# One exponential a pair of score banks, with the 16-bit part cast on GpSimd

## What is computed

```python
x = x + attention(group_norm(x))        # layer 0
x = x + likelihood(group_norm(x))       # layer 1
# attention: q, k = prelu(1x1 conv to 24 channels), v = prelu(1x1 conv to 192 channels)
score = softmax(einsum('bnc,bcm->bnm', q, k), axis=2)      # 4096 x 4096 an image
out = einsum('bnm,bmc->bnc', score, v)
# likelihood: a small per-channel network (1-3-3-3-1, tanh) of x - 0.5 and x + 0.5
likelihood = maximum(abs(sigmoid(sign * upper) - sigmoid(sign * lower)), 1e-6)
```

## Time and profile before

| what | value |
|---|---|
| median of 3 runs | 5428.71 us (5420.52 to 5429.87) |
| the profiled execution, its own time | 5432.77 us |
| its span | 5430.7 us |
| mean granted clock of TensorE | 0.942 |
| instructions | 105319 |
| chain of work that ended last, by engine | TensorE 56%, ScalarE 12%, DMA 11%, issue 11%, VectorE 8%, GpSimd 1% |

### The profile page before, as it was taken

How to read it: one execution, slowest core, us unless ns; L and a number is a source line. 1 busy time by engine, 2 the same in 40 slices (tenths; PEclk the granted TensorE clock), 3 DMA queues, 4 the chain that set the end, 5 groups by cost and what they waited for, 6 DMA issues and landing times.

```text
span 5430.7 us, 105319 instructions
## 1 busy us (share of the span) xinstructions
PE 4730.2 (87%) x38408; PEld 3138.7 (58%) x38408; DVE 4132.9 (76%) x5378; ACT 3765.9 (69%) x4149; POOL 805.6 (15%) x934
## 2 busy tenths in 40 slices
PE   4999779998899977999789997899878998789966
PEld 2877327773378723886248762588525885267821
DVE  4887578966888667886678867788577885789855
ACT  1666786667866687666876668766687666876677
POOL 5200320003200132001310013100221002210012
PEclk8999899998999899998999989999899998899988
DMA  2101440014300143001430024200242002420033
GB/s 56 26 19 30 106 110 18 13 38 108 100 18 19 37 117 89 16 19 43 121 81 13 19 56 118 71 19 15 68 120 56 19 19 74 118 53 14 19 99 94
DMA packets 107342, 305.21 MB, mean 56 GB/s; under 512 B 14401, under 2 KB 14785, under 8 KB 105090
## 3 DMA queue, kind: packets, MB, share of 16 engines
q1 hardware_dynamic: 106818, 298.01, 20.6%
HBM read 230.65 MB, written 50.33 MB: 52 GB/s over the span
## 4 chain that ended last, share of the span: by engine, by line
PE 56%; ACT 12%; DMA 11%; issue 11%; DVE 8%; SPq 1%; POOL 1%; DVEq 0%; ACTq 0%; POOLq 0%
PE ps L1270 10%; PE ps L1272 10%; PE ps L1274 10%; DMA arena<-x2d 7%; PE ps L1058 7%; PE ps L1221 6%; ACT th L627 5%; PE ps L1085 4%; ACT arena L620 3%; DVE mxp L958 3%; PE ps L1132 2%; PE ps L1115 2%; PE ps L1146 2%; DMA qst<-shared 2%; DVE arena L953 2%
## 5 line engine op out<-in xcount | busy, mean ns | idle before, releaser
L1272 PE MATMUL ps<-v_sb,arena 128*128 128x192 f16 x8192 | 2039.7, 249 | 0.0
L1270 PE MATMUL ps<-v_sb,arena 128*128 128x193 f16 x8192 | 2031.2, 248 | 8.7 <-DVE arena L953 8.7
L1274 PE MATMUL ps<-v_sb,arena 128*128 128x193 f16 x8192 | 2022.7, 247 | 0.0
L577 ACT ACTIVATE arena<-ps 128x1024 f16<-128x1024 f32 x1024 | 1049.5, 1025 | 1018.2 <-PE ps L1058 1017.9
L953 DVE TENSOR_TENSOR arena<-arena 128x1024 f16<-128x1024 f32 x1024 | 1247.8, 1219 | 281.5 <-ACT arena L580 280.1
L958 DVE TENSOR_REDUCE mxp<-ps 128x1 f32<-128x512 f32 x1792 | 1188.1, 688 | 124.6 <-PE ps L1221 113.2
L900 DVE SCALAR_TENSOR_TENSOR th<-th,gates,ps 128x1024 f32<-128x1024 f32 x768 | 953.7, 1277 | 428.1 <-ACT th L627 426.4
L580 ACT ACTIVATE arena<-ps 128x1024 f32<-128x1024 f32 x1024 | 1045.9, 1021 | 0.0
L1272 PEld LDWEIGHTS ps<-v_sb,arena 128*128 128x128 f16 x8192 | 801.0, 98 | 265.3 <-issue 4.7
L627 ACT ACTIVATE th<-ps,biases 128x1024 f32<-128x1024 f32 x768 | 821.6, 1118 | 158.7 <-PE ps L1132 124.3
L1270 PEld LDWEIGHTS ps<-v_sb,arena 128*128 128x128 f16 x8192 | 798.2, 97 | 145.7 <-issue 22.1
(11 more groups left out here) (122 smaller groups left out, 3528.6 us busy)
## 6 DMA issues: line engine op xcount, KB each, us to landing
arena<-x2d SPq DMA_DIRECT2D x384, 256.0 KB
arena<-x2d SPq DMA_DIRECT2D x384, 128.0 KB, 3.8
xp<-x_dram SPq DMA_DIRECT2D x18, 1536.0 KB, 15.2
shared<-x_dram SPq DMA_DIRECT2D x64, 384.0 KB, 3.6
x2d<-shared SPq DMA_DIRECT2D x64, 384.0 KB, 3.1
res<-x2d SPq DMA_DIRECT2D x96, 256.0 KB
out_dram<-res SPq DMA_DIRECT2D x96, 256.0 KB
kst<-shared SPq DMA_DIRECT2D x32, 256.0 KB, 11.2
```

Source lines behind the costliest of these rows:

```text
L577: act.activation(e_hi[:, q % 4, :].rearrange("p (k n) -> p k n", k=2), sc, ACT.Exp)
L1270: pe.matmul(acc, eh, v_sb[:, m, 0:C + 1], start=(m == 0 and t % 2 == 0), stop=False, skip_group_check=True)
L1272: pe.matmul(acc[:, 0:C], eh, v_sb[:, m, VW:VW + C], start=False, stop=False, skip_group_check=True)
L1274: ins = pe.matmul(acc, el, v_sb[:, m, 0:C + 1], start=False, stop=(m == MT - 1), skip_group_check=True)
```

## The change

ScalarE takes one exponential of each pair, the 32-bit one, into `e_32`, which now has four slots (`ER`). GpSimd reads it and writes the 16-bit part `e_hi` with a cast (`high`). GpSimd now has a `phase_b` of its own. It waits for the exponential (`full_ready`) and, from the fifth pair on, for the pair four before to be used up (`summed`); it signals `hi_ready`. VectorE's `low` waits for `hi_ready` instead of `full_ready`. ScalarE waits for `lo_ready` of the pair four before only. TensorE's program is unchanged: it waits for `full_ready` and `lo_ready` at the same places. The three steps of the last layer-1 unit on GpSimd move from the end of its phase A to pairs 1, 3 and 5 of its new phase B, each behind the cast of that pair.

```diff
+ER = 4
...
-        e_32 = arena[:, 8 * N:12 * N].rearrange("p (s n) -> p s n", s=2)
+        e_32 = arena[:, 8 * N:16 * N].rearrange("p (s n) -> p s n", s=ER)
...
@@ GpSimd, phase_a @@
-                    if l is not None and 0 <= u < UNITS:
+                    if l is not None and 0 <= u < (UNITS - 1 if proj else UNITS):
...
+            def high(pairs, q):
+
+                full, free = pool.compute_val(pairs + (q + 1)), pool.compute_val(pairs + (q - 3))
+                settle(pool)
+                pool.wait_ge(full_ready, full)
+                if q >= 4:
+                    pool.wait_ge(summed, free)
+                pool.tensor_copy(e_hi[:, q % 4, :], e_32[:, q % ER, :]).then_inc(hi_ready, 1)
+
+            def phase_b(b, l):
+                def body(before, first, final):
+                    pairs = pool.compute_val(b * BLOCKS * PAIRS + before * PAIRS)
+                    for p in range(PAIRS):
+                        if p + 2 < PAIRS or not final:
+                            high(pairs, (0 if first else PAIRS) + p + 2)
+                        if first and l is not None:
+                            if p == 1:
+                                sums(l, UNITS - 1)
+                            if p == 3:
+                                signs(l, UNITS - 1)
+                            if p == 5:
+                                difference(l, UNITS - 1)
+
+                for q in range(2):
+                    high(pool.compute_val(b * BLOCKS * PAIRS), q)
+                body(0, True, False)
+                with pool.Fori(0, (BLOCKS - 2) // 2) as jj:
+                    body(pool.compute_val(jj * 2), False, False)
+                    body(pool.compute_val(jj * 2 + 1), False, False)
+                body(BLOCKS - 2, False, True)
...
@@ ScalarE, exps @@
-                if q >= 4:
-                    act.wait_ge(summed, pairs + (q - 3))
-                act.activation(e_hi[:, q % 4, :].rearrange("p (k n) -> p k n", k=2), sc, ACT.Exp)
-                if q >= 2:
-                    act.wait_ge(lo_ready, pairs + (q - 1))
-                act.activation(e_32[:, q % 2, :].rearrange("p (k n) -> p k n", k=2), sc,
+                if q >= ER:
+                    act.wait_ge(lo_ready, pairs + (q - ER + 1))
+                act.activation(e_32[:, q % ER, :].rearrange("p (k n) -> p k n", k=2), sc,
                                ACT.Exp).then_inc(full_ready, 1)
...
@@ VectorE, low @@
-                    dve.wait_ge(full_ready, pairs + (q + 1))
-                    dve.tensor_tensor(e_lo[:, q % 4, :], e_32[:, q % 2, :], e_hi[:, q % 4, :],
+                    dve.wait_ge(hi_ready, pairs + (q + 1))
+                    dve.tensor_tensor(e_lo[:, q % 4, :], e_32[:, q % ER, :], e_hi[:, q % 4, :],
                                       ALU.subtract).then_inc(lo_ready, 1)
```

More of the change, by code:

```diff
@@ L242, in program @@
         full_ready = sem("full_ready")
+        hi_ready = sem("hi_ready")
         lo_ready = sem("lo_ready")
@@ L481, in coefficients, with sums, signs, difference @@
                 ins.then_inc(set_gp, 1)
+            def sums(l, u):
+                pool.wait_ge(lu_ready, l * UNITS + u + 1)
+                if u >= 1:
+                    pool.wait_ge(signed_ready, l * UNITS + u)
+                pool.tensor_tensor(lu_sign[:, :], lu[:, u % 2, 0, :], lu[:, u % 2, 1, :], ALU.add
+                                   ).then_inc(sum_ready, 1)
+            def signs(l, u):
+                pool.wait_ge(sign_ready, l * UNITS + u + 1)
+                pool.tensor_tensor(lu[:, u % 2, 0, :], lu[:, u % 2, 0, :], lu_sign[:, :], ALU.mult)
+                pool.tensor_tensor(lu[:, u % 2, 1, :], lu[:, u % 2, 1, :], lu_sign[:, :], ALU.mult
+                                   ).then_inc(signed_ready, 1)
+            def difference(l, u):
+                pool.wait_ge(sig_ready, l * UNITS + u + 1)
+                pool.tensor_tensor(lu[:, u % 2, 0, :], lu[:, u % 2, 1, :], lu[:, u % 2, 0, :], ALU.subtract
+                                   ).then_inc(dif_ready, 1)
             def phase_a(l, proj):
@@ L503, in values @@
                                        ALU.subtract).then_inc(v_done, 1)
[L505 to L521, removed]
                 if proj:
@@ L531, in phase_a @@
                     u = (s - 5) // 4
-                    if l is not None and 0 <= u < UNITS:
+                    if l is not None and 0 <= u < (UNITS - 1 if proj else UNITS):
                         if (s - 5) % 4 == 0:
-                            sums(u)
+                            sums(l, u)
                         if (s - 5) % 4 == 1:
-                            signs(u)
+                            signs(l, u)
                         if (s - 5) % 4 == 2:
-                            difference(u)
+                            difference(l, u)
+            def high(pairs, q):
[25 more added lines that the diff above has]
+                body(BLOCKS - 2, False, True)
             phase_a(None, True)
             coefficients()
-            with pool.Fori(0, B - 1) as b:
-                phase_a(b, True)
+            phase_b(0, None)
+            with pool.Fori(0, B - 1) as l:
+                phase_a(l, True)
+                phase_b(pool.compute_val(l + 1), l)
             phase_a(B - 1, False)
```

## The result

The changed kernel takes 5523.4 us (median of 4 runs, 5519.9 to 5526.9) against 5426.4 us before: ratio 1.018, 95% interval 1.0162 to 1.0197. That is outside the range of 5429 to 5470 us and 3.6 times the loss of 27 us that was forecast.

What follows compares the result with a forecast made beforehand. TensorE, not ScalarE, was taken as the bound in attention, with VectorE also full in pairs with maxima. 8 x 1.0 + 7 x 0.9 + 8 x 1.6 = 27.1 us gave 5459.9 us profiled, 5455 us median; range 5429 to 5470 us.

Steps and rivals of the forecast that it cites:

- Cast 1.03 us: The added 128x1024 cast on GpSimd takes 1.03 us, extrapolated from smaller casts; 2.0 us kept as the other bound.
- Full pairs unchanged, cover of the chain 0.8 us: Pairs with three maxima stay 3.08 us apart; in pairs without maxima the longer exponential-to-low chain has 0.8 us to spare.
- In short pairs, cast plus low want 2.25 us of 2.43 us: tight, but it fits: In pairs without maxima, the port shared by VectorE and GpSimd has room for cast and low; no loss.
- What is queued in front of the cast on GpSimd: Sum, sign products and difference of the last unit stand between casts; low, then TensorE's products, wait for the cast.
- (b): First block with a previous image, 7 times: low 5 meets GpSimd's second sign product, +0.9 us each.
- (a): Start of phase B, 8 times: cast 1 takes the port before low 0, +1.0 us each; otherwise +0.1 us.
- (c): Last block after the square root's table loads, 8 times: cast 9 goes before low 8, +1.6 us; otherwise +0.4 us.
- Low up to 2.2 us, TensorE behind low near 25 us: Signs: low's maximum rises from 1.41 us, some 20 to 30 times; TensorE's wait for low rises from 8.7 us.
- Port throughput in short pairs: Rival, chance 0.10: casts nearer 1.5 us overfill pairs without maxima, 118 us at most, about 5500 us.
- Low ahead: Rival, chance 0.25: low takes the port before the cast at phase B's start and in last blocks; 10.3 us, 5439.
- no change: Rival, chance 0.12: the port costs nothing, as sign products fall differently or VectorE's four-maxima pairs have slack; 5429 to 5433.
- Faster: Rival, chance 0.08: at phase B's start and in last blocks TensorE gains the removed exponential's 0.9 us; 14 us, 5414.

Runs made afterwards that it cites:

- middle: Changed kernel, GpSimd's cast of pair 13 held back, both exponentials on ScalarE in every image's first and last blocks (last: pairs 2 to 15): 5416.7 us, ratio 0.9999.
- wait13: Changed kernel, with GpSimd's cast of pair 13 held back until the maxima are split, in all blocks but an image's last: 5496.3 us, ratio 1.0125.
- idle casts: Kernel before, plus on GpSimd a 960-column cast of a constant tile per pair that nobody waits for: 5453.6 us, ratio 1.0056.
- first block: Changed kernel, with both exponentials on ScalarE for pairs 0 to 15 of image 0 alone: 5494.9 us, ratio 1.0131.

## Why the prediction was wrong

The direction was right, the size was not: 27 us were forecast, 97 us came (89 us between the two profiled executions, 5521.7 - 5432.8). About 51 us of the 89 stood at nothing in the prediction: 26 us of straight blocks and 25 us of image 0's start. Point by point.

- **Cast 1.03 us:** right, 1.04 us where alone. Mean 1.12 us, in the forecast band. GpSimd 1927 us (about 1900), ScalarE 2831 us (some 2720; it counted the overlap of two neighbouring exponentials twice).
- **Full pairs unchanged, cover of the chain 0.8 us:** right. Exponentials of full pairs are 3.08 us apart (906.78 to 909.86 in the second image). Straight blocks without the collision take 47.6 us as before, and middle and wait13 show the cover.
- **The failed step: "In short pairs, cast plus low want 2.25 us of 2.43 us: tight, but it fits", and then three places only.** The port paragraph asked which instructions of VectorE meet the cast and looked at low alone. I dismissed the maxima as PSUM reads and never listed the other VectorE instructions of a block. Pair 11 has no maxima, so it is a short pair, but VectorE splits the maxima in it. The third step of the split met the cast of pair 13 and took 0.98 us for 0.17 us, and TensorE's transpose and next scores came 0.8 us later. The prediction put this at nothing; it is 25.9 us in straight blocks. wait13 takes back 26 us there, and TensorE's wait before the transpose went from 7.3 to 47.2 us and back to 3.2 us. With other timing other steps meet the cast: in idle casts the fourth and the sixth step took 0.89 and 0.91 us once each.
- **What is queued in front of the cast on GpSimd:** named only for the last layer-1 unit. This term, too, stood at nothing. `coefficients` stands between phase A and the new phase B of image 0, and its instructions are in the trace of the kernel before until 167 us, while low starts at 133.0. 25 us, shown by first block.
- **(b), 0.9 us an image:** the mechanism was right, one meeting of three. The lows of 2.02 and 2.06 us are the same price at two arrivals that I did not follow. With (a) the forecast was 1.9 us a first block; it was 4.4 us. TensorE's wait for the maxima rose by 17 us, where 6 us were forecast.
- **(a), the race:** cast 1 won. TensorE's first products in the second image wait 2.52 us instead of 0.41 us, while its wait before the scores fell from 3.57 to 2.65 us: +1.2 us together, 1.0 us forecast.
- **(c), 1.6 us:** 2.0 us measured. The casts went ahead as assumed. Steps of the group norm meet casts as well, as at 1193.66 (0.97 us for two columns), but no run tells how much of the rest is theirs.
- **Low up to 2.2 us, TensorE behind low near 25 us:** 2.32 us and 59.0 us, of which 26.7 us is image 0's start; without it 32 us. It took over 1.5 us 53 times, where 20 to 30 were forecast.
- **Port throughput in short pairs, 118 us, rival:** its total is near the measured loss, but it is not what happened. It needs a cast of 1.2 us or more where alone, and that one took 1.04 us. In wait13 straight blocks have all their casts in short pairs and take what they took before. That this rival's number lies closer is luck.
- **Low ahead and no change, rivals:** fell, by (a) and by the time.
- **Faster, rival:** fell. ScalarE's backlog at (a) did clear earlier and low was late next.

The 14 us that phase A gained stay open. The seven experiments, whose phase A is nearly that of the changed kernel, have 1861 to 1883 us there, so 14 us is no more than these differ among themselves. TensorE's wait for layer 1's inputs (behind DMA) does not follow it: 152.4 us before and 125.8 us after, but 151.8 us in wait13, whose phase A is shorter than before, too. I did not test whether GpSimd's shorter queue there helps.

## What to carry to other kernels

Before work goes to an idle engine that shares a port, list every instruction of the sharing engine in the stretch, down to the ones of 0.17 us: a small one in front of a handoff to another engine can pay all that is left of the big one that it meets. Small instructions that take many times their usual time beside the other engine may already be in the trace before the change, as L837 was. Read, too, what the new consumer's queue has to finish before its first item, in the first iteration as well as in the steady one. And here, relief of an engine whose idle time was ended by the bound engine was worth 0.0%, in the version where nothing else was disturbed (middle).

## What the runs showed of the hardware

A VectorE `tensor_scalar` on 128x4, one SBUF input, waits out a GpSimd cast: 0.98 us instead of 0.17 us. So does a VectorE `tensor_tensor` on 96x2, both inputs in SBUF (0.97 us instead of 0.16 us). VectorE's reductions from PSUM do not: their mean is 0.688 us before and after, though most of the 1792 run beside a cast in the changed kernel. Nor does its `bn_stats` on an SBUF tile, 96x512: 0.69 us at 926.74 beside the cast of 926.58, as before. A semaphore increment that GpSimd issues without an instruction of its own passed while at least 5.7 us of its earlier instructions had not yet run (152.6 against 158.4).
